# Bias add on GpSimd: sixteen instructions of 128x256 per pair of blocks in place of eight of 128x512

## The reference

```python
xn = layernorm(x)                                  # over the 512 features
s = einsum('btd,dm->btm', xn, Win) + bin_          # M = 64
h = relu(s[..., None] * W1 + b1)                   # 16 hidden values for each of the 64
g = einsum('btmh,mh->btm', h, W2) + b2
out = einsum('btm,md->btd', g, Wout) + bout
x = x + attention(xn) + out                        # attention acts on the first 16 tokens of each batch,
                                                   # and adds the row bo on every token
```

## Time and profile before

| | |
|---|---|
| median of 3 runs | 303.3 us |
| the profiled execution | 303.48 us, its span 301.7 us |
| granted TensorE clock, mean | 0.979 |
| PE busy | 276.4 us (92%) |
| DVE busy | 251.3 us (83%) |
| POOL busy | 234.0 us (78%), of them 160.5 in the bias adds |
| ACT busy | 219.9 us (73%) |
| DMA moved | 87.87 MB, mean 291 GB/s |

### The profile page before, as it was taken

How to read it: one execution, slowest core, us unless ns; L and a number is a source line. 1 busy time by engine, 2 the same in 40 slices (tenths; PEclk the granted TensorE clock), 3 DMA queues, 4 the chain that set the end, 5 groups by cost and what they waited for, 6 DMA issues and landing times.

```text
span 301.7 us, 6220 instructions
## 1 busy us (share of the span) xinstructions
PE 276.4 (92%) x2371; PEld 116.1 (38%) x2371; DVE 251.3 (83%) x392; ACT 219.9 (73%) x260; POOL 234.0 (78%) x209
## 2 busy tenths in 40 slices
PE   4797498989999999899999999999989999999990
PEld 4652265524443432434443434434343333242220
DVE  0878484999997799998599987899999989967682
ACT  1546733873788699797979778898769797976910
POOL 8543109999679797979897897979793989899940
PEclk9999689997999999999999999999999999999998
DMA  7999979997988799999899999999799999450688
GB/s 239 284 369 393 255 189 333 342 347 285 262 302 250 238 360 290 389 283 386 194 319 296 335 343 294 357 267 406 171 357 302 354 314 333 126 233 37 240 241 336
DMA packets 50573, 87.87 MB, mean 291 GB/s; under 512 B 6360, under 2 KB 35184, under 8 KB 46448
## 3 DMA queue, kind: packets, MB, share of 16 engines
q1 hardware_dynamic: 46400, 65.96, 70.4%
q10 hardware_dynamic: 3504, 21.37, 20.2%
q0 software_dynamic: 640, 0.16, 0.8%
HBM read 53.77 MB, written 33.69 MB: 290 GB/s over the span
## 4 chain that ended last, share of the span: by engine, by line
PE 61%; DVE 23%; issue 6%; POOL 3%; DMA 3%; ACT 1%; DVEq 0%; POOLq 0%; ACTq 0%
PE sg L594 14%; PE sg L537 13%; PE op L629 12%; DVE x L1048 6%; DVE stats L1092 5%; PE ra L556 4%; PE ra L629 3%; DMA b2c<-in_L_ffn_b_dram 3%; DVE xqT L1079 2%; PE op L352 2%; PE rb L483 1%; PE op L483 1%; PE ra L483 1%; PE ra L352 1%; PE A L326 1%
## 5 line engine op out<-in xcount | busy, mean ns | idle before, releaser
L1227 POOL TENSOR_TENSOR x<-x,bias_row 128x512 f32<-128x512 f32 x128 | 160.5, 1293 | 0.0
L1092 DVE BATCH_NORM_STATS2 stats<-x 128x6 f32<-128x512 f32 x128 | 80.7, 672 | 9.5 <-DMA x<-in_L_attn_x_dram 9.5
L816 ACT ACTIVATE H<-ra,b1c,w1c 128x1024 f32<-128x1024 f32 x64 | 72.8, 1205 | 9.4 <-PE rb L556 9.3
L816 ACT ACTIVATE H<-rb,b1c,w1c 128x1024 f32<-128x1024 f32 x60 | 68.9, 1220 | 3.0 <-PE sg L594 2.5
L594 PE MATMUL sg<-H,w2s 128*32 128x512 f32 x496 | 64.6, 616 | 3.0 <-ACT H L816 2.9
L1048 DVE TENSOR_TENSOR x<-x,op 128x1024 f32<-128x1024 f32 x46 | 55.7, 1212 | 13.3 <-PE op L629 13.2
L1211 POOL TENSOR_TENSOR rstd<-veps,nhalf 128x8 f32<-128x8 f32 x16 | 26.7, 1671 | 43.0 <-DVE veps L1104 42.9
L537 PE MATMUL sg<-xT,win 128*32 128x512 f32 x256 | 58.0, 595 | 1.3 <-ACT xqT L787 0.9
L629 PE MATMUL op<-wout,G 64*128 64x512 f32 x184 | 51.6, 637 | 2.2 <-DVE x L1048 1.9
L537 PE MATMUL sg<-xqT,winq 128*32 128x512 f32 x224 | 50.8, 595 | 0.0
L1079 DVE STREAM_TRANSPOSE xqT<-xq 128x1024 f32<-128x1024 f32 x28 | 34.6, 1234 | 2.2 <-DMA xq<-in_L_attn_x_dram 2.1
(11 more groups left out here) (203 smaller groups left out, 358.5 us busy)
## 6 DMA issues: line engine op xcount, KB each, us to landing
out_dram<-x SPq DMA_DIRECT2D x30, 1024.0 KB, 6.8
x<-in_L_attn_x_dram ACTq DMA_DIRECT2D x10, 2048.0 KB, 10.5
xq<-in_L_attn_x_dram SPq DMA_DIRECT2D x112, 128.0 KB, 6.1
x<-in_L_attn_x_dram SPq DMA_DIRECT2D x12, 1024.0 KB, 11.9
out_dram<-x SPq DMA_DIRECT2D x4, 512.0 KB, 4.9
x<-in_L_attn_Wq_dram SPq DMA_DIRECT2D x1, 1024.0 KB, 19.0
x<-in_L_attn_Wk_dram SPq DMA_DIRECT2D x1, 1024.0 KB, 21.1
x<-in_L_attn_Wv_dram SPq DMA_DIRECT2D x1, 1024.0 KB, 7.4
```

The lines of the kernel that those rows point to most:

```text
L816: act.activation(Hr[half][k % len(Hr[half])][:, :], rep_ps[half][:, :], ACT.Relu, bias=b1c[:, half, k:k + 1], scale=w1c[:, half, k:k + 1]) ...
L1092: dve.bn_stats(stats[:, j, :], x_sb[m][:, j * D:(j + 1) * D]).then_inc(bn_done, 1)
L1227: pool.tensor_tensor(x_sb[m][:, c], x_sb[m][:, c], bias_row[:, :], ALU.add).then_inc(xc_done, 1)
```

## The change

Each bias add on POOL is cut in two along the columns: in place of one instruction on 128x512 there are two on 128x256, each with its half of bias_row. xc_done is raised by each of them, so the count that DVE waits for is doubled. Nothing else is touched.

```diff
@@ def add(n, j)
-            dve.wait_ge(xc_done, TPP * n + 2 * j + 2)
+            dve.wait_ge(xc_done, 2 * (TPP * n + 2 * j + 2))
@@ def add_bias(n, i)
-            c = slice(j * D, (j + 1) * D)
-            pool.tensor_tensor(x_sb[m][:, c], x_sb[m][:, c], bias_row[:, :], ALU.add).then_inc(xc_done, 1)
+            for f in range(2):
+                c, d = slice(j * D + f * D // 2, j * D + (f + 1) * D // 2), slice(f * D // 2, (f + 1) * D // 2)
+                pool.tensor_tensor(x_sb[m][:, c], x_sb[m][:, c], bias_row[:, d], ALU.add).then_inc(xc_done, 1)
```

## The result

The changed kernel took 306.33 us (median of 4, 305.14 to 306.93) against 303.3 for the kernel before in the same runs (303.25 to 303.71): a ratio of 1.0091, 95% interval 1.0069 to 1.0114. It is slower by about 3 us where I had forecast 1.9 us faster, and it lies 0.8 above my range. The profiled execution has 305.14 us and a span of 303.4.

What follows compares the result with a forecast made beforehand. The chain ending last was 61% PE, 23% DVE, 3% POOL, so the change could act only through engines POOL makes wait. 303.48 - 2.0 - 0.8 + 0.8 = 301.5, stated as 301.4 us; range 299.3 to 305.5.

Steps and rivals of the forecast that it cites:

- Price of a short piece: POOL's 256-column adds: 0.16 us fixed per instruction, so one every 0.70 us in place of 1.24.
- Gain 1: 52 to 76 us: shorter DVE stalls shrink PE's 1.50 us stand and avoid the clock fall; everything behind 2.0 us earlier.
- more gain: Rival, chance 0.12: spacing near 0.65, PE not held for rwide(3), gain at 52 to 76 us is 3, no collisions; 299.6.
- Gain 2: Near 224 us: two DVE ops stand 1.1 us less together, so PE's 0.81 us wait goes; 0.8 us gained.
- Loss once per block: Each block: 1.3 us more POOL, covered first by its wait for veps; 0.8 us charged in all, in attention blocks.
- The waits for veps: Sign to look for: POOL's waits for DVE's veps before pow fall from 42.9 us to some 28.
- The collisions of variance instructions: In the tightest blocks m and dm meet running pieces, 0.8 us of delay; 0.2 to 0.3 us charged three times.
- Letting in at each end: Stalled DVE ops get in whenever a POOL instruction ends, so halving the adds halves this wait.
- a rival with a chance of 0.08: DVE gets in only where POOL's queue has a hole; stalls stay 1.3 us, POOL's 1.3 us per block is paid: 303.5 to 306.
- The tail: End of kernel: POOL's small DMAs have 18 us until the span's end, so a shift of one or two costs nothing.

Runs made afterwards that it cites:

- the repetition: The changed kernel run again without further edits, against the kernel before: 303.06 us, median of 12, ratio 0.9999 (0.9969 to 1.003).
- the isolated kernels: Small kernels without the real computation: POOL runs of 512-, 256- or 128-column adds beside small DVE probe instructions; adds took 1.22, 0.68 and 0.41 us each.
- the kernels with the product: Kernel before plus one unread 128x512 POOL product per pair: 305.74 us in all pairs, 305.37 in the first 13; four behind the last add: 304.35.

## Why the prediction was wrong, by its own steps

- *Price of a short piece*, 0.70 us a piece with 0.16 fixed: right. 0.69 in the kernel, 0.68 in isolation, 0.14 fixed.
- *Gain 1*, 2.0 us: right in size and path. Variance instructions at 0.66 to 0.80 us, the stand of PE down to 0.37, no fall of the clock, PE waiting for rwide next, replicate 2.02 us nearer. Where fewer pieces stand ahead of pow(3) it is 3.2, which is the 3 of the rival *more gain*.
- *Gain 2*, 0.8 us: PE's 0.81 is gone in both profiles, but the stretch is 0.70 shorter only in the one in which L1006 was let in at the next end, and 0.07 in the other. Why is open.
- *Loss once per block*, 0.8 us in all: 1.11 us, but at one place, L984 at 80 us, and by a mechanism that I did not have. The waits for veps fell to 33.9 us, not 28, and in the kernel with only the later pairs split the stretch from 76 to 278.6 is even 1.2 us shorter. The collisions of variance instructions that I charged cost nothing that is seen.
- *Letting in at each end*: this step failed. From the 1.23 and 1.34 us between chained instructions I concluded that DVE is let in whenever a POOL instruction ends, and so that shorter pieces can only shorten its waits. It is so beside 512-column adds and in most cases beside 256. But an instruction can be passed over until the run is over, which is 2.98 us on the path at 193 us (L1006, 4.88 us long) and, by inference, some 5 at 62. I had this as a rival with a chance of 0.08, and in it the stalls stay at 1.3 us; that they could grow to the length of POOL's run was in no case. All evidence that I had was of instructions that were let in at once and of their followers.
- *The tail*: "a shift of one or two is nothing there" failed. The shift was 4.2 us, 2.3 of it from the last 32 pieces and the rest from their later start, and it costs 0.8 to 1.3 us in the profiles and 1.1 in the run that does only this. I had looked at the room up to the end of the span and not at what else is on the DMA engines in it.

Summed: -2.0 + 1.1 + 3.0 + 0.8 is 2.9 us, 306.4 for an execution with the passing over at 193 us, and -2.0 + 1.1 - 0.7 + 1.3 is -0.3, 303.2 for one without. The two groups of the repetition, medians 303.0 and 306.2, lie there. POOL's added time is in both sums: gain 1 is 3.2 with four tiles split and 2.0 with all, and the tail is the rest. It is why even the short executions are no faster than the kernel before; the 3 us between the groups are L1006 in the one long execution that has a profile. That all four executions of the first measurement were of the long kind and three of twelve of the second is not explained, and that the other long ones are long by L1006 too is not shown.

The Trainium skill ("SBUF — State Buffer", Who interferes with whom) gives the shared port pair to whoever issues first, for the whole instruction. The wait of one piece fits that. The 4.88 us beside pieces of 0.69 does not follow from it, since six instructions of POOL had ended before the one whose end let L1006 in.

What stays open is why an instruction is passed over. It happened to dmean, L984, L1006 and L1021, in the profiles never to an instruction that directly followed one just let in. The profiles give a hint, no more. Beside pieces of 256 columns back to back, L984, L1006 and the dmean near 260 us began 0.02 to 0.13 us after the end of a piece. Others that began there were let in at the next end (L955 after 0.01, veps after 0.05 to 0.06), so the phase alone doesn't tell the cases apart. None of some 800 probes was passed over, but beside 256 columns none of them began in the first 0.09 us after an end, so the isolated kernels leave that window untested; beside 128 columns they reach it. In the profiled executions with first pairs split and no waits, all but one of them short, dmean at 62 us began 0.04 to 0.08 us before an end: a shift of some 0.1 us would put it into that window. Whether that makes the long executions is not tested.

## What to carry to other kernels

An instruction of DVE that shares its port with a run of short POOL instructions has no guarantee of the next gap. Split only the POOL instructions that a critical DVE instruction meets, and put a wait of POOL for its own result behind them. Price the rest of a split at 0.14 us for each added instruction, and ask at each place where POOL itself is awaited (here pow at 67 us and the end) what a later POOL moves; the waits belong in that price. Where executions fall into two groups, a median and one profile tell of one of them; look at all times.

## What the hardware showed that I had not expected

- A DVE instruction of 8 columns can last 7.35 us (256-column pieces with memsets) or 10.60 us (128-column pieces) beside back-to-back POOL instructions, to the end of their run or within 0.4 us of it; beside 512-column adds DVE's small instructions take at most 1.37 us in the kernel before and 1.46 in the kernels with the product, about one add.
- A one-column memset between the pieces doesn't let DVE in (the 7.35 us above). A wait of POOL for its own last piece does, and costs 0.12 us a piece (0.81 against 0.69 with it behind all of them).
- Eight accumulating DMAs of 16 KB from POOL make four stores of 512 KB land 0.9 to 1.4 us later when they coincide (5.8 to 6.3 us in the kernels with a late POOL, 6.0 in the one that only delays them, against 4.9).
